# One ScalarE copy moved ahead of a Silu pair in the skewed steps of an audio tower kernel

## The reference, cut to what matters

```python
conv = conv1d(x, kernel)               # 9 taps, 64 -> 128 channels, 248 tokens per sequence
h = relu(tanh(conv * scale) + bias)    # scale: from the norm of each window of x
h = h + mamba2(layernorm(h))           # projection, 4-tap causal conv, Silu, scan over time,
                                       # gate, RMS norm, projection back
h = h + ffn(layernorm(h))              # 16 experts, top 2, a shared expert, a last MLP
```

## Time and profile before

| | |
|---|---|
| median of 3 runs | 1053.64 us (1052.08 to 1056.99) |
| profiled execution | 1052.6 us, of which the span (first to last instruction) is 1050.8 us |
| TensorE busy | 915.5 us, 87% |
| VectorE busy | 725.7 us, 69% |
| ScalarE busy | 501.0 us, 48% |
| GpSimd busy | 587.3 us, 56% |
| mean granted TensorE clock | 0.937 |

### The profile page before, as it was taken

How to read it: one execution, slowest core, us unless ns; L and a number is a source line. 1 busy time by engine, 2 the same in 40 slices (tenths; PEclk the granted TensorE clock), 3 DMA queues, 4 the chain that set the end, 5 groups by cost and what they waited for, 6 DMA issues and landing times.

```text
span 1050.8 us, 22359 instructions
## 1 busy us (share of the span) xinstructions
PE 915.5 (87%) x6324; PEld 797.8 (76%) x6325; DVE 725.7 (69%) x2092; ACT 501.0 (48%) x1259; POOL 587.3 (56%) x649
## 2 busy tenths in 40 slices
PE   3697999999999999999878449999999998759998
PEld 3576777877777787777756348999999998748887
DVE  5357788787887888788886235555565554599993
ACT  3333554445544545445431214555555554546654
POOL 5435355766777676677754734444444444445652
PEclk9989999999999999899986567999999999969999
DMA  7300000100001100000055411222222221133432
GB/s 177 85 11 11 1 11 11 31 23 26 18 26 30 32 21 23 18 21 20 13 143 182 136 30 51 83 84 75 66 64 56 60 65 51 48 95 92 114 97 51
DMA packets 72056, 59.12 MB, mean 56 GB/s; under 512 B 19168, under 2 KB 61467, under 8 KB 71984
## 3 DMA queue, kind: packets, MB, share of 16 engines
q1 hardware_dynamic: 63440, 41.88, 15.2%
q0 software_dynamic: 8544, 16.34, 4.7%
HBM read 35.62 MB, written 23.81 MB: 57 GB/s over the span
## 4 chain that ended last, share of the span: by engine, by line
PE 39%; DVE 21%; issue 20%; POOL 12%; ACT 5%; another core or an unknown queue 1%; DMA 1%; SPq 0%; DVEq 0%; POOLq 0%; ACTq 0%
PE psum L967 13%; PE psum L952 13%; POOL x_slots L1362 5%; DVE arena L1852 4%; DVE arena L1504 2%; DVE arena L1512 2%; POOL rs L1345 2%; PE psum L785 2%; DVE arena L1857 2%; PE psum L961 2%; POOL arena L1338 2%; PE psum L650 1%; ACT arena L1064 1%; POOL arena L1313 1%
## 5 line engine op out<-in xcount | busy, mean ns | idle before, releaser
L1189 ACT ACTIVATE arena<-psum,arena 128x128 f32<-128x128 f32 x556 | 159.0, 369 | 154.7 <-PE psum L952 134.1
L1395 POOL DMA_INDIRECT y_tokens<-arena x139 | 137.3, 988 | 161.0 <-DVE arena L1802 117.6
L952 PE MATMUL psum<-arena 128*128 128x128 f32 x1112 | 154.6, 284 | 24.0 <-DVE arena L1795 12.9
L952 PEld LDWEIGHTS psum<-arena 128*128 128x128 f32 x1112 | 140.0, 198 | 26.2 <-issue 12.8
L967 PE MATMUL psum<-arena 128*128 x1112 | 156.6, 284 | 0.4 <-issue 0.4
L1362 POOL DMA_INDIRECT x_slots<-arena,idx x128 | 127.8, 999 | 34.5 <-issue 34.5
L967 PEld LDWEIGHTS psum<-arena 128*128 128x128 f32 x1112 | 138.0, 195 | 7.6 <-issue 1.0
L1789 DVE COPY arena<-arena 128x644 f32 x139 | 76.2, 548 | 72.3 <-issue 67.0
L1795 DVE TENSOR_SCALAR arena<-psum,lng,lnb 128x128 f32<-128x128 f32 x139 | 56.9, 409 | 52.6 <-PE psum L961 41.0
L1504 DVE TENSOR_TENSOR_SCAN arena<-psum,arena 124x496 f32<-124x496 f32 x64 | 72.6, 1175 | 29.7 <-PE psum L785 26.3
L1332 POOL TENSOR_TENSOR arena<-arena 128x496 f32<-128x496 f32 x32 | 39.8, 1244 | 42.7 <-DVE arena L1532 42.7
(11 more groups left out here) (283 smaller groups left out, 2229.8 us busy)
## 6 DMA issues: line engine op xcount, KB each, us to landing
arena<-x_slots SPq DMA_DIRECT2D x139, 64.5 KB
arena<-y_tokens SPq DMA_DIRECT2D x16, 448.0 KB
arena<-in_x SPq DMA_DIRECT2D x16, 256.0 KB, 3.0
out_tokens<-arena SPq DMA_DIRECT2D x16, 224.0 KB
y_tokens<-arena POOLq DMA_INDIRECT x139
x_slots<-zero_src SPq DMA_DIRECT2D x33, 64.5 KB, 3.2
moe_all<-in_x SPq DMA_DIRECT2D x4, 512.0 KB, 5.9
x_slots<-arena,idx POOLq DMA_INDIRECT x128
```

Source lines behind the costliest of these rows:

```text
L952: last = nc.tensor.matmul(psum[:, 2 + b.q % 2, k * 128:(k + 1) * 128], w1_blk[b.q % 4][:, k * 128:(k + 1) * 128], hT[b.q % 2], start=True, ...
L1189: last = nc.scalar.activation(EHT[t.q % 2][:, k * 128:(k + 1) * 128], psum[:, 2 + t.q % 2, k * 128:(k + 1) * 128], ACT.Silu, bias=w1_blk[t ...
L1395: nc.gpsimd.indirect_dma_start(out=y_tokens, out_offset=bass.IndirectOffsetOnAxis(ap=xb[t.q][:, F:F + 1].bitcast(i32), axis=0), in_=YO[t.q ...
```

## The change

ScalarE's list for a step has two entries in the other order: `convT_copy(a)` now stands ahead of `bc_silu(b)`. No instruction is added or removed, and the lists of the other engines are the same.

```diff
                     if d is not None: normed(d)
                     if b is not None: silu(b, 0)
                     if d is not None: stage(d)
+                    if a is not None: convT_copy(a)
                     if b is not None: bc_silu(b)
-                    if a is not None: convT_copy(a)
                     if d is not None: hhT_copy(d)
                     if a is not None: tanh(a); relu(a)
```

## The result

| | before | after |
|---|---|---|
| median | 1052.86 us (1048.22 to 1056.99, 4 runs) | 1024.17 us (1022.65 to 1033.73, 4 runs) |
| profiled execution, span | 1052.6, 1050.8 us | 1024.98, 1023.1 us |
| mean granted TensorE clock | 0.937 | 0.945 |

The ratio is 0.9736 (95% interval 0.9691 to 0.978): 28.7 us less, where 25.7 were forecast from the profiled execution, which itself got 27.6 us shorter. The time lies in the range, and by 0.2 us within its likeliest part, 1024 to 1032.

A forecast was written before the change was run, and what follows sets the result against it. No engine is busy throughout a step; a loop of waits through ScalarE's late copy was taken to bound it. -18.7 - 1.0 + 0.4 - 6.4 = -25.7 us takes 1052.6 to 1026.9, put at 1028; range 1023 to 1038.

The forecast's parts named there:

- The wait of L693: TensorE's transposes wait for the copy in steps 3 to 15; each step shortens by its wait, -18.7 us in all.
- Step 2 and step 1: Step 2 loses its wait, -1.0 us; in step 1 the Silus wait behind the copy and delay the tanh, +0.4 at most.
- The clock: Two falls of TensorE's clock in steps 3 to 15 go once the gap is filled, -6.4 us; other bound 0.
- The rival in which the falls stay: The waits go but both clock falls in steps 3 to 15 remain: sum -19.3, 1034.3 us; chance 0.27.
- the slower one: More clock falls in the shorter steps, each 3.2 us; one in all 13 steps gives 1069.5 us; chance 0.04.
- The covers: Idle time on ScalarE, VectorE and GpSimd was to let each step keep its whole 1.44 us gain.
- VectorE's wait before L1504: VectorE's 1.76 us wait for the decays of L785 shrinks by 1.44 to 0.32, passing the gain on whole.
- L1311's: GpSimd's idle time before L1311, after gate and decay, shrinks by 0.88, from 1.21 to 0.33 us.
- the thinnest cover: GpSimd's idle time before L1311; without it up to 0.88 of each 1.44 us would be lost.

The follow-up runs named there:

- late_copy_filled: late_copy plus fifteen transposes where TensorE waits for the copy in steps 3 to 15; 1057.34 us against 1051.88 for the kernel before, ratio 1.0023.
- step1_old: The changed kernel with the old order of convT_copy and bc_silu in step 1 alone; 992.86 us in one run.
- fill_transpose: The kernel before with nine transposes, output unread, where TensorE waits for the copy in steps 3 to 15; 1019.41 us against 1027.32, ratio 0.9943.
- late_copy: The kernel before with convT_copy moved the other way, behind hhT_copy; 1077.66 us against 1027.32, ratio 1.0513.
- after_third: The changed kernel run a third time, unaltered, on a fast chip; 992.51 us against 1027.48 for the kernel before, ratio 0.9685.
- late_tanh: The changed kernel with residual_input(d) moved from the step's end to ahead of the tanh, steps 3 to 15; 994.96 us against 992.51.

## Why the prediction was right, point by point

**The wait of L693 sets the step.** Right. It was forecast at 18.7 us for steps 3 to 15; the lead grows by 1.50 per step, 13 x 1.50 = 19.5. The extra 0.06 per step is overlap: without a wait the transposes start 0.07 us before the work ahead of them ends, and the idle time in the trace does not count that. That no engine gives it back is shown by late_copy_filled, which moved the wait the other way and lost 0.8 of 0.8.

**Step 2 and step 1.** -1.0 and +0.4 were forecast. From step 1 to step 3 the lead went from 0.48 to 2.56; less the 1.50 of step 3's own wait, that is -0.6 for the two together, as forecast. That the tanh of step 1 is 0.4 us late is shown by step1_old; that the chain carries it on whole rests on this sum.

The Trainium skill (TensorE: Matmul & The Clock Gate, Part 1, Architectural detail) calls ScalarE strictly first in, first out; the trace of step 1 agrees, where the Silus ran at 40.63 in the old order and at 43.42 in the new, behind the copy.

**The clock.** Right in sign and size, -6.4 forecast and -6.3 found, and now shown to come from the gap: filled with work that changes nothing, it has no falls (fill_transpose), lengthened by 0.8 us it has them in every step (late_copy), and filled again none (late_copy_filled). The rival in which the falls stay is out; so is the slower one. Why the falls of before come in just two of the steps, the same two in both profiles, is open; the forecast took their number from the row and did not derive it.

The Trainium skill (the same page, Part 4, PE-mode transpose) would have had transposes keep the clock up less than matmuls do. Here nine transposes per step, 1.1 us of them, did it as well as nine matmuls, with no fall in steps 3 to 15 in either: for this filler the measurement differs from the page.

**The covers.** This was the weak step. VectorE's wait before L1504 was forecast at 0.32 us and L1311's at 0.33. In steps 3 to 5 they are 0.26 and 0.22, in later ones of this profile 0.5 to 0.7, though the steps are no longer for it; in after_third they stay at 0.26 and 0.2. And I had called L1311 the thinnest cover, without which up to 0.88 of each 1.44 us would be lost. late_tanh took it away, and of what TensorE lost, 0.0 or 0.3 us per step, nothing came by way of L1311. The weak step is that I followed the tanh only to the first engine that waits, and not on to TensorE, which has time left there. It did no harm, since the cover held.

**What the sum lacks.** 27.7 us of span against 25.7 forecast: 0.5 lay ahead of step 1's L693, 0.8 in the waits and about 0.8 behind step 15. No step of the prediction bears on the first and the last. The clock falls there too, and the start of step 1's L693 varies from 42.3 to 44.3 us between the profiles, so both may be chance. The waits alone were mis-sized, by the 0.06 per step. That the median moved by 28.7 and not 27.6 lies in the spread of the runs.

## What to carry to other kernels

Where an engine waits in a list written by hand, look at what stands behind the wait with its data ready: here one copy stood 2.7 us behind two Silus, and TensorE stood 1.4 us behind the copy. Follow the gain along the loop until TensorE takes it or not, and past the first idle time that covers it. Small gaps of TensorE cost twice where the clock falls behind them, so a gap that looks harmless is to be priced with the falls that come after it, and a cheap filler tells how many of them it causes.

## What the runs showed of the hardware

- A wait of 1.44 us per step had a fall of the clock behind it in 2 of 13 steps, each of 6.8 us at half clock. One of 2.23 us at the same place had a fall behind it in all 13, of 6.8 or some 10 us, at 4.2 us per step on average. So what the clock cost rose from 0.5 to 4.2 us per step while the gap grew by 0.8.
- Nine fp32 transposes of 128 columns filled 1.44 - 0.3 = 1.14 us, 0.13 each; nine fp32 matmuls with the same operands took 1.44 + 0.55 = 1.99, 0.22 each, and stand in the trace as eighteen.
- The same program ran in two speeds on different chips. The transposes of the expert loop (L961) went from 569.8 to 880.6 us in the first profile of the changed kernel, 310.8 us, from 573.5 to 878.4 in the second, 304.9, and from 567.4 to 848.2 on a fast chip, 280.8 us, with steps of equal length in the first part. Which operation makes the difference was not looked into.
- In both profiles of the changed kernel on slower chips L1504 started some 0.4 us later behind the decays of L785 from step 6 on (1.51 us after the start of L785 instead of 1.09). In that of after_third, on a fast chip, it did not. The cause is open; the steps are no longer for it.
